# Destination blocks aligned to half groups in a four-layer graph network kernel

## The chip, the cores and the metric

The kernel runs on one core of a Trainium2 chip. The metric is the device time of one execution in microseconds (us). Three executions of the kernel before took 2282.65, 2286.11 and 2288.14 us; the median, 2286.11, is its time. A separate, profiled execution took 2289.18 us. The engines are PE (matrix products), DVE (vector), ACT (scalar functions), POOL (general, here also the issuer of indirect DMAs) and SP (issuer of plain DMAs). Each works through its own list of instructions, and semaphores order them among each other.

## The reference

A graph of 625 nodes with 512 features each and 20,000 edges goes through four layers. Each is `x = x + layer(relu(layernorm(x)))`. Cut to what each does with the edges:

```
# layer 0: mean over incoming edges, then one product
mean = segment_sum(x[src], dst) / max(count, 1)
out  = concat(x, mean) @ W.T + b
# layer 1, twice: relational convolution, 4 bases, 8 relations
m    = sum_b comp[etype, b] * (h @ basis[b])[src] * norm
out  = segment_sum(m, dst) + bias + h @ loop_w
# layer 2: tensor product messages, 1024 numbers for an edge
tpw  = silu-MLP(edge_attr_8) @ W4            # four weights of 128
m    = concat(w1*s0*y0, w4*<s1,y1>/sqrt3, w2*s0*y1, w3*s1*y0)
out  = lin(segment_sum(m, dst))
# layer 3: edge MLP, 512 numbers for an edge
h    = mish(concat(x[src], x[dst], edge_attr_64) @ W1 + b1)
agg  = segment_sum(mish(h @ W2 + b2), dst)
y    = layernorm(x + mish(concat(x, agg) @ W3 + b3) @ W4 + b4)
```

## The kernel before, in words

**Blocks, slots, tiles, groups.** The 625 nodes are 5 blocks (`NB`) of 125 (`BN`). The edges are sorted by the block of their destination; each edge gets a slot. A tile is 128 slots, a group (`TG` = 4 tiles, `SG` = 512 slots) is what layers 2 and 3 handle at a time. Each block's slots begin at a multiple of `SG`, so that all edges of a group end in one block, and there are `NG` = 44 groups, `NT` = 176 tiles. `block_of_group` says for each group which block it is; the pass reads it with a value load and adds to that block of `total`. An edge's record (80 floats: attributes, weight, source, destination) is written to its slot in `sorted_records` by an indirect DMA that POOL issues, one for each of 160 columns of 125 edges (`scatter_records`, L677 to L682). Only half of the records fit on chip at a time: columns 0 to 79 (`EARLY`) first, and the late ones come in by `late_records` on SP into the same room, after the early ones that stood there are scattered.

**Stages.** They follow each other, each in an `nc.Block()`; an engine's list in a stage is written out in the kernel, and the places below in that list are the order of the work.

- `place_edges` (to 65 us in the profiled execution): counts by bucket, slots, `block_of_group`.
- `order_pairs` (65 to 207): lists (source, destination) pairs for layers 0 and 1. Meanwhile POOL issues 64 of the scatters (`FIRST`, L482), then waits for `placed` and clears the tail of `pairs` (L484). DVE computes the layer norm's statistics of x (L656 to L663) in the middle of its last loop.
- `build_pairs` (207 to 403): the pair matrices. SP brings in late records of columns 0 to 63.
- `layer0` (403 to 467), `normalize` (to 480). POOL in layer 0: L1149, five scatters, five adds of a bias (L1154), eleven scatters.
- `relation_conv` twice (480 to 625.5, 625.5 to 792). In the first (c = 0) POOL issues the 80 late scatters, and SP loads the late records of columns 64 to 79 before its conv weights (L1281 to L1284). The second (c = 1) turns the sorted records into transposed attributes, in `UNITS` = 22 units of 8 tiles (L1450 to L1457 on DVE, L1394 on ACT, L1337 and L1384 on PE), beside its matrix products.
- `message_pass` (816 to 1321, layer 2), `edge_tables` (to 1387) and `edge_mlp_pass` (1387 to 2186, layer 3), `node_tail`.

**Message pass.** For each tile k of a group g, PE computes four path weights (`path_weights`, L1641 to L1643, bf16), one layer of the next group's MLP (`layer`, L1634, k < 3), and `scatter` (L1653, L1655): fp32 products of a one-hot matrix `hot` (slot to node of the block) with the message of 1024 columns, summed in PSUM over the group's four tiles in `sum_ps[g % 2]`. DVE makes the products for the messages from PSUM and the gathered rows (`paths`: L1745, L1750, L1756), the products with the record's vector and their sum over three components (`turn` L1721, `inner_first` L1729, `inner_second` L1734), `hot` (L1712), and adds the finished sum of group g-1 to `total` after tile 1 (`add`, L1769). ACT scales four pieces for each tile (L1689) and does the MLP's silu (L1682). POOL copies a group's source rows (L1601) and gathers them by four indirect DMAs (L1607), two groups ahead, in a ring of four.

**Edge pass.** A group has two units of two tiles. PE builds the first layer's input from `by_dst` rows of the group's block times the columns `hotT` (L1918), from the attributes (L1919, L1920) and the gathered source rows (L1923), multiplies by `w2` (L932), and scatters (L1946), summing over both units. DVE makes `hotT` by a comparison (`hot_columns`, L2022), `hot` (L2027), the mish pieces (L2035, L2040, L2046, L2058) and one add for each group (`add`, L2067). ACT does the exponentials and logarithms; POOL the low parts (L1873, L1878) and gathers.

Of the kernel before, what the change touches and what calls it, by code (L numbers as in the profile page):

```python
# [12 lines left out]
FP32 = mybir.dt.float32  # L13
# [14 lines left out]
SG = TG * P  # L28
RING = 4
NG = (EDGES + NB * (SG - 1)) // SG  # L30
NG += -NG % RING
# [14 lines left out]
FIRST = 64  # L46
# [23 lines left out]
def constants(pg):  # L70
# [19 lines left out]
    pg.block_of_group = pg.sb("block_of_group", [1, NG], I32)  # L90
# [37 lines left out]
    pg.scattered = pg.keep.enter_context(nc.semaphore("record_scattered"))  # L128
    pg.arrived = [pg.keep.enter_context(nc.semaphore(f"arrived{b}")) for b in range(RING * TG)]
# [31 lines left out]
def place_edges(pg):  # L161

    nc = pg.nc
    with ExitStack() as ctx:
# [18 lines left out]
        groups = pg.sb("groups", [P, NB], ctx=ctx)  # L183
        last_group = pg.sb("last_group", [P, NB], ctx=ctx)
# [4 lines left out]
        group_no = pg.sb("group_no", [P, NG], ctx=ctx)  # L189
        group_blk = pg.sb("group_blk", [P, NG], ctx=ctx)  # L190
        group_past = pg.sb("group_past", [P, NB - 1, NG], ctx=ctx)
# [11 lines left out]
                "rows_counted", "rows_summed", "ints_read", "weight_read", "weight_rounded", "weight_part", "weight_left", "tables_made", "tables_turned", "group_compared")}  # L203
# [25 lines left out]
        def _(pool):  # L229
# [6 lines left out]
            nc.gpsimd.iota(group_no[:, :], [[1, NG]], base=0, channel_multiplier=0,  # L236
                           allow_small_or_imprecise_dtypes=True).then_inc(sem["iota_done"], 1)
            pool.wait_ge(sem["group_compared"], 1)
            nc.gpsimd.tensor_tensor(group_past[:, 0:2, :], group_past[:, 0:2, :], group_past[:, 2:4, :],
                                    ALU.add).then_inc(sem["group_compared"], 1)  # L240
            pool.wait_ge(sem["group_compared"], 2)
            nc.gpsimd.tensor_tensor(group_blk[:, :], group_past[:, 0, :], group_past[:, 1, :],
                                    ALU.add).then_inc(sem["group_compared"], 1)
            pool.wait_ge(sem["group_compared"], 3)
            nc.gpsimd.tensor_copy(pg.block_of_group[:, :], group_blk[0:1, :])
            nc.gpsimd.tensor_copy(pg.block_of_tile[:, :].rearrange("p (g k) -> p g k", k=TG),
# [160 lines left out]
def order_pairs(pg):  # L407
# [8 lines left out]
    with ExitStack() as ctx:  # L416
# [2293 lines left out]
```

## Time and profile before

| stretch (us) | stage | length | PE busy | DVE busy | ACT busy | POOL busy |
|---|---|---|---|---|---|---|
| 0 to 65 | constants, place_edges | 65 | 1.7 | 52.8 | 12.9 | 8.3 |
| 65 to 207 | order_pairs | 142 | 106.6 | 115.5 | 78.5 | 115.1 |
| 207 to 403 | build_pairs | 196 | 158.5 | 171.8 | 151.1 | 146.5 |
| 403 to 480 | layer0, normalize | 77 | 60.2 | 55.1 | 14.0 | 45.5 |
| 480 to 625.5 | first convolution | 145.5 | 137.9 | 49.4 | 23.8 | 112.7 |
| 625.5 to 792 | second convolution | 166.5 | 147.8 | 59.9 | 42.8 | 0.0 |
| 816 to 1321 | message pass | 505 | 494.7 | 427.4 | 262.0 | 216.7 |
| 1387 to 2186 | edge pass | 799 | 769.4 | 709.4 | 550.6 | 679.1 |
| 2186 to 2287 | node tail | 101 | 66.2 | 27.7 | 22.2 | 12.5 |

The profiled execution took 2289.18 us; its span, from the first to the last instruction, is 2287.4 us, and the mean clock that PE was granted was 0.959 of full speed. A timeline row gives the start, the busy time, the engine, the line, the operation, what it writes and reads with shapes, the number of instructions taken together, and in brackets the idle time before it and what ended it. In the table of stretches a busy time is the engine's own within the stretch; time in which an indirect DMA is prepared by POOL counts as busy, the gap of about 0.3 us between two of them does not.

### The profile page before, as it was taken

To read this page: it belongs to the slowest core of one execution; us is meant where nothing else is said; L and a number is where in the kernel's file an instruction comes from. 1 tells how busy PE (TensorE), PEld (TensorE's weight loads), DVE (VectorE), ACT (ScalarE), POOL (GpSimd) and SP (SyncE) were. 2 spreads that over 40 slices of the span, in tenths; PEclk is the share of its full clock that TensorE was granted. 3 is DMA by queue.
4 is the path that set the end of the run, shared out by engine and by line. 5 is a ranking of instruction groups with operands and counts; after the bars stand their busy time and mean duration, and the time that the engine had idled before them with its cause. 6 is when DMAs were issued, how large, how long until landed. Compare 5 with 4: busy or idle time off the path is not lost. (4 is left out here: it accounts for less than half of the span.)

```text
span 2287.4 us, 35553 instructions
## 1 busy us (share of the span) xinstructions
PE 2009.2 (88%) x11336; PEld 1132.4 (50%) x11456; DVE 1708.3 (75%) x2399; ACT 1178.9 (52%) x1952; POOL 1349.6 (59%) x1068
## 2 busy tenths in 40 slices
PE   0894888879998779999999987999999999999875
PEld 0773777446565534444444453545555554555332
DVE  8995998743333558888888845999999999999623
ACT  1664777121122225555555524777677767777522
POOL 1787777747600054444444105898998989899530
PEclk9997999889999879999999999999999999999987
DMA  2411000222144245333333214322222222222000
GB/s 116 163 21 59 0 0 0 72 82 69 33 119 122 70 123 157 116 94 94 94 98 96 50 33 133 114 72 78 72 78 70 81 76 71 73 77 77 1 0 23
DMA packets 81683, 170.25 MB, mean 74 GB/s; under 512 B 17383, under 2 KB 43226, under 8 KB 80579
## 3 DMA queue, kind: packets, MB, share of 16 engines
q0 software_dynamic: 35840, 98.88, 16.0%
q1 hardware_dynamic: 45754, 70.25, 9.3%
q8 instruction: 48, 0.79, 0.1%
q14 instruction: 41, 0.34, 0.0%
HBM read 144.93 MB, written 23.98 MB: 74 GB/s over the span
## 5 line engine op out<-in xcount | busy, mean ns | idle before, releaser
L932 PE MATMUL e_two_ps<-w,e_first 128*128 128x512 bf16 x1342 | 405.4, 380 | 4.0 <-issue 0.2
L680 POOL DMA_INDIRECT sorted_records<-edge_record,slot_row x160 | 248.2, 1551 | 84.0 <-issue 55.2
L1689 ACT ACTIVATE u_msg<-u_t,slot_record 128x128 f32<-128x128 f32 x704 | 223.3, 390 | 93.2 <-DVE u_t L1745 93.1
L2349 POOL DMA_INDIRECT e_got<-src_table,e_idx x176 | 227.9, 1295 | 70.4 <-issue 34.8
L932 PE MATMUL e_two_ps<-w,e_first_low 128*128 128x512 bf16 x685 | 260.2, 380 | 0.6
L1873 POOL TENSOR_TENSOR e_first_low<-e_first 128x1024 bf16<-128x1024 f32 x88 | 248.4, 2823 | 12.6 <-DVE e_first L2046 12.6
L1607 POOL DMA_INDIRECT u_got<-up_table,u_idx x176 | 186.4, 1059 | 76.8 <-issue 42.9
L1878 POOL TENSOR_TENSOR e_msg_low<-e_act 128x1024 bf16<-128x1024 f32 x88 | 200.6, 2279 | 38.0 <-DVE e_act L2058 36.5
L932 PEld LDWEIGHTS e_two_ps<-w,e_first 128*128 128x128 bf16 x1408 | 134.4, 98 | 148.4 <-issue 2.2
L734 PE MATMUL pairs_ps<-cell_high,src_hot 128*128 128x144 bf16 x1180 | 153.6, 227 | 60.7 <-POOL cell_rest L758 38.6
L1653 PE MATMUL u_sum_ps<-u_msg,u_hot 128*125 128x512 f32 x352 | 185.2, 608 | 3.2 <-ACT u_msg L1689 3.1
L1655 PE MATMUL u_sum_ps<-u_msg,u_hot 128*125 128x512 f32 x352 | 180.6, 595 | 0.0
L2053 DVE TENSOR_TENSOR e_lin<-e_two_ps,bias 128x512 f32<-128x512 f32 x176 | 120.4, 684 | 63.6 <-PE e_two_ps L932 63.6
L2035 DVE SCALAR_TENSOR_TENSOR e_act<-e_act 128x1024 f32<-128x1024 f32 x88 | 160.9, 1828 | 5.9 <-ACT e_act L1971 5.9
L1976 ACT ACTIVATE e_act<-e_lin 128x1024 f32<-128x1024 f32 x88 | 93.0, 1057 | 125.0 <-DVE e_lin L2053 125.0
L1980 ACT ACTIVATE e_act<-e_act,log_bias 128x1024 f32<-128x1024 f32 x88 | 101.1, 1148 | 107.9 <-DVE e_act L2035 107.9
L734 PEld LDWEIGHTS pairs_ps<-cell_high,src_hot 128*128 128x128 bf16 x1180 | 115.8, 98 | 76.8 <-POOL cell_rest L758 74.5
L737 PE MATMUL pairs_ps<-cell_rest,src_hot 128*128 128x128 f16 x1180 | 153.1, 221 | 0.0
L1601 POOL COPY u_idx<-src_row 128x4 uint32<-128x4 uint32 x44 | 26.0, 592 | 194.4 <-DVEq L1760 171.1
L1436 DVE TENSOR_TENSOR pairs<-rc_mix,pairs 125x512 bf16<-125x512 f32 x40 | 27.7, 692 | 146.9 <-ACT pairs L1404 146.9
L1358 PE MATMUL rc_out<-pairs 125*125 125x512 bf16 x600 | 135.6, 379 | 1.2
L1682 ACT ACTIVATE u_hid<-u_mlp_ps 128x256 f32<-128x256 f32 x132 | 50.5, 383 | 146.4 <-PE u_mlp_ps L1634 146.4
(373 smaller groups left out, 4726.9 us busy)
## 6 DMA issues: line engine op xcount, KB each, us to landing
conv_w<-in_L_gnn_basis_dram SPq DMA_DIRECT2D x8, 1024.0 KB, 5.6
sorted_records<-pairs SPq DMA_DIRECT2D x5, 1408.0 KB, 10.9
later_w<-in_L_gnn_W_dram SPq DMA_DIRECT2D x6, 1024.0 KB
attr_parts<-h SPq DMA_DIRECT2D x22, 256.0 KB, 2.1
e_attrT<-attr_parts SPq DMA_DIRECT2D x44, 128.0 KB
e_dst_all<-dst_row SPq DMA_DIRECT2D x44, 125.0 KB
edge_record<-in_edge_floats_dram SPq DMA_DIRECT2D x1, 3125.0 KB
pairs<-in_edge_floats_dram SPq DMA_DIRECT2D x1, 3125.0 KB
```

The source lines that it names most:

```text
L680: pg.nc.gpsimd.indirect_dma_start(out=pg.sorted, out_offset=bass.IndirectOffsetOnAxis(ap=pg.slot_row[:, j:j + 1], axis=0), in_=pg.edge_rec ...
L734: nc.tensor.matmul(ps[h][:, sb, 0:(COEFS + 1) * CELL], hot, high[:, h, k, :, :].rearrange("p n d -> p (n d)"), start=(k == 0 and sb % 2 == ...
L737: last = nc.tensor.matmul(ps[h][:, sb, 0:COEFS * CELL], hot, rest[:, h, k, :, :].rearrange("p n d -> p (n d)"), start=False, stop=(k == 1 ...
L932: last = nc.tensor.matmul(out, lhsT, rhs, start=(n == 0), stop=(n == len(pairs) - 1))
L1607: nc.gpsimd.indirect_dma_start(out=got[:, b, :], out_offset=None, in_=tableU, in_offset=bass.IndirectOffsetOnAxis(ap=idx[:, r, k:k + 1], a ...
L1653: nc.tensor.matmul(sum_ps[h][0:BN, 0:D], hot[:, h * TG + k, :], msg[:, k, 0:D], start=(k == 0), stop=(k == TG - 1))
L1655: nc.tensor.matmul(sum_ps[h][0:BN, D:M], hot[:, h * TG + k, :], msg[:, k, D:M], start=(k == 0), stop=(k == TG - 1)).then_inc(scattered, 1)
L1689: last = nc.scalar.activation(msg[:, k, at * MUL:(at + 1) * MUL], t12[:, k % 2, of], ACT.Copy, scale=pg.record[:, bass.ds(t, 1), Y + m])
L1873: nc.gpsimd.tensor_tensor(first_low[:, r % 2, 2 * u:2 * u + 2, :], full, upper(full), ALU.subtract).then_inc(low1, 1)
L1878: nc.gpsimd.tensor_tensor(msg_low[:, u, :, :], act2[:, u, :, :], upper(act2[:, u, :, :]), ALU.subtract).then_inc(low2, 1)
L2035: nc.vector.scalar_tensor_tensor(out=act1[:, u, :, :], in0=act1[:, u, :, :], scalar=2.0, in1=act1[:, u, :, :], op0=ALU.add, op1=ALU.mult). ...
L2349: pg.nc.gpsimd.indirect_dma_start(out=self.got[:, r * TG + k, :], out_offset=None, in_=table, in_offset=bass.IndirectOffsetOnAxis(ap=self. ...
```

## The change

Blocks are aligned to a half group, 256 slots (`HG`), so a group's first and second half may belong to two blocks. The worst case needs fewer slots: `NG` = 42 groups (84 halves, `NH`), 168 tiles, 21 units in the second convolution. What depends on the block is now by half: `block_of_half`, the sums of the message pass (`sum_ps[k // 2]`, two tiles each), the sums of the edge pass (`sum_ps[u]`, one unit each), and the edge pass's rows by destination, which are taken in two products of 256 columns where one of 512 was.

In the message pass ACT copies each half group's sum from PSUM to `part` (`take_sum`), after tiles 0 and 2, and POOL adds `part` to `total` (`add`), after its gathers 0 and 2; DVE's add is gone. In the edge pass DVE adds for each unit, and ACT makes `hotT` by an absolute value and a relu (`hot_columns`), where DVE compared. The loop by four groups becomes `group_by_group`, which the message pass used already.

In the ordering stage POOL issues 52 scatters (`FIRST`) and its clear of the tail goes to ACT; DVE's statistics of x move ahead of its wait for `placed`. Layer 0 then has the bias adds first and 12 scatters (to `BESIDE` = 64), and the first convolution 16 + 52 + 28 = 96. SP there loads the weights 1 and 2 before the late records. Late scatters count on a semaphore of their own.

```diff
+TH = TG // 2
+HG = TH * P
-NG = (EDGES + NB * (SG - 1)) // SG
-NG += -NG % RING
+NH = (EDGES + NB * (HG - 1)) // HG
+NG = -(-NH // 2)
+NH = 2 * NG
-FIRST = 64
+FIRST = 52
+BESIDE = 64
...
 # order_pairs, POOL
             scatter_records(pg, range(0, FIRST))
-            pool.wait_ge(placed, 1)
-            nc.gpsimd.memset(pairs[:, HOTS:], 0.0)
 # order_pairs, ACT
+            act.wait_ge(placed, 1)
+            clear(pairs[:, HOTS:])
...
 # layer0, POOL
-            scatter_records(pg, range(FIRST, FIRST + 5))
             pool.wait_ge(bias_in, 16)
             for b in range(NB):
                 nc.gpsimd.tensor_tensor(pg.x[:, b, :], pg.x[:, b, :], bias[:, :], ALU.add).then_inc(biased, 1)
-            scatter_records(pg, range(FIRST + 5, EARLY))
+            scatter_records(pg, range(FIRST, BESIDE))
...
 # relation_conv, c == 0, SP
-                sp.wait_ge(pg.scattered, 16 * EARLY)
-                late_records(pg, sp, FIRST, EARLY)
                 for m in range(1, BASES + 2):
                     load_conv_weight(pg, room, sp, m)
+                    if m == 2:
+                        sp.wait_ge(pg.scattered, 16 * EARLY)
+                        late_records(pg, sp, FIRST, EARLY)
...
 # relation_conv, c == 0, POOL
+                scatter_records(pg, range(BESIDE, EARLY))
                 pool.wait_ge(pg.record_in, 16)
                 scatter_records(pg, range(EARLY, EARLY + FIRST))
...
 # message_pass, POOL
+            def add(n):
+                at = nc.gpsimd.value_load(pg.block_of_half[0:1, bass.ds(n, 1)], min_val=0, max_val=NB - 1)
+                pool.wait_ge(summed, n + 1)
+                if n >= 1:
+                    pool.wait_ge(added, n)
+                into = total[:, bass.ds(at, 1), :].rearrange("p a d -> p (a d)")
+                nc.gpsimd.tensor_tensor(into, into, part[:, n % 2, :], ALU.add).then_inc(added, 1)
...
                 for k in range(TG):
                     if more:
                         gather((r + 2) % RING, k)
+                    if k == 0 and at > 0:
+                        add(2 * g - 1)
+                    if k == 2:
+                        add(2 * g)
...
 # message_pass, PE
+                if k % TH == 0 and g >= 1:
+                    pe.wait_ge(summed, 2 * (g - 1) + k // TH + 1)
                 if k == 0:
-                    pe.wait_ge(added, g + 1)
                     pe.wait_ge(hot_ready, g + 1)
...
 # message_pass, ACT
+            def take_sum(n):
+                act.wait_ge(scattered, TH * (n + 1) + 2 * TG)
+                if n >= 2:
+                    act.wait_ge(added, n - 1)
+                nc.scalar.copy(part[:, n % 2, :], sum_ps[n % 2][0:BN, :]).then_inc(summed, 1)
...
                 for k in range(TG):
                     vector_paths(g, r % 2, k)
                     if k < 3 and at < LAST:
                         layer(g + 1, 1 - r % 2, k)
+                    if k == 0 and at > 0:
+                        take_sum(2 * g - 1)
+                    if k == 2:
+                        take_sum(2 * g)
...
 # message_pass, DVE
-                    if k == 1 and at > 0:
-                        add(g - 1, 1 - r % 2)
...
 # edge_mlp_pass, PE
                     for part in range(2):
-                        rows = by_dst[:, bass.ds(at, 1), part, cols].rearrange("p b d -> p (b d)")
-                        nc.tensor.matmul(ps, rows, hotT[:, h, :], start=(part == 0), stop=False)
+                        for half, at in enumerate(blocks):
+                            rows = by_dst[:, bass.ds(at, 1), part, cols].rearrange("p b d -> p (b d)")
+                            slots = slice(half * HG, (half + 1) * HG)
+                            nc.tensor.matmul(pre_ps[u][:, i, slots], rows, hotT[:, h, slots],
+                                             start=(part == 0 and half == 0), stop=False)
...
 # edge_mlp_pass, ACT
+                if u == 0 and at + 3 < NG:
+                    hot_columns(g + 3, (r + 3) % 2)
+
+            def hot_columns(g, h):
+                act.wait_ge(attr_in[h], (g - h) * 16 + 32)
+                act.wait_ge(pre_ready, 2 * g - 2 + 2 * RING)
+                nc.scalar.activation(off_lane[:, h, :], dst_all[:, h, :], ACT.Abs,
+                                     bias=gathers.minus_lane[:, 0:1]).then_inc(offs_made, 1)
+                act.wait_ge(offs_made, g + 1)
+                nc.scalar.activation(hotT[:, h, :], off_lane[:, h, :], ACT.Relu, bias=pg.ones[0:BN, 0:1],
+                                     scale=-1.0).then_inc(hotT_ready, 1)
```

## Rows read from the trace of the kernel before

**Rows 1.** The profile page's first line.
```profile
span 2287.4 us, 35553 instructions
```

**Rows 2.** Busy us (instructions): PE, PEld, DVE, ACT, POOL; granted clock, DMA share, GB/s.
```profile
480.00:625.50 145.50, 137.85 (x620) 86.11 (x620) 49.41 (x44) 23.82 (x32) 112.74 (x80) 0.96 0.24 64
...
816.00:1321.00 505.00, 494.69 (x1466) 227.85 (x1496) 427.37 (x838) 261.97 (x837) 216.72 (x221) 0.98 0.36 102
...
1387.00:2186.00 799.00, 769.44 (x4487) 388.57 (x4576) 709.43 (x660) 550.61 (x529) 679.11 (x385) 0.99 0.26 74
```

**Rows 3.** Timeline of the ordering stage: start, us, instruction [idle before <- releaser].
```profile
155.69 0.40 DVE L605 COPY h<-pair_slots_ps 128x236 f32<-128x236 f32 x1 [3.30 <-PE pair_slots_ps L514]
175.18 3.06 DVE L656 BATCH_NORM_STATS2 x_stats<-x 125x6 f32<-125x512 f32 x5
186.91 0.64 DVE L673 TENSOR_TENSOR pair_rest<-hT,pair_high 128x472 f16<-128x472 f32 x1
199.19 4.25 POOL L484 MEMSET pairs<- 128x4960 f32 x1
207.31 0.83 ACT L769 ACTIVATE src_off<-iota_src,hT 128x640 f16<-128x640 f16 x1 [21.19 <-ACTq L765]
```

**Rows 4.** Layer 0: the queries of line L1169, and POOL's timeline.
```profile
L1169 DVE TENSOR_TENSOR w<-w x2: 2598/4989/7380, 411.3 to 419.3; 128x2048 bf16<-128x2048 f32 x2
  PEld first_out L1106: 2.4, 1
...
417.97 6.24 POOL L1154 TENSOR_TENSOR x<-x,bias 125x512 f32<-125x512 f32 x5
```

**Rows 5.** Timeline of POOL and DVE at both ends of the first convolution.
```profile
480.62 1.19 POOL L680 DMA_INDIRECT sorted_records<-edge_record,slot_row  x1 [27.41 <-DMA edge_record<-in_edge_floats_dram]
...
621.03 1.19 POOL L680 DMA_INDIRECT sorted_records<-edge_record,slot_row  x1 [0.30 <-issue]
624.55 0.68 DVE L1493 TENSOR_TENSOR hT<-rc_mix,hT 128x500 bf16<-128x500 f32 x1 [1.00 <-ACT hT L1413]
```

**Rows 6.** Timeline of DVE at the last unit of the second convolution.
```profile
777.41 0.43 DVE L1450 CAST h<-edge_record 128x512 bf16<-128x512 f32 x1 [2.46 <-PE attr_ps L1337]
```

**Rows 7.** Timeline of the message pass, one group; then the add of two groups.
```profile
1010.87 1.12 PE L1653 MATMUL u_sum_ps<-u_msg,u_hot 128*125 128x512 f32 x2
1016.13 0.59 PE L1634 MATMUL u_mlp_ps<-u_hid,u_w 128*128 128x256 f32 x2
1018.93 1.02 PE L1653 MATMUL u_sum_ps<-u_msg,u_hot 128*125 128x512 f32 x2
1016.76 0.38 ACT L1682 ACTIVATE u_hid<-u_mlp_ps 128x256 f32<-128x256 f32 x1 [1.25 <-PE u_mlp_ps L1634]
1017.04 1.26 ACT L1689 ACTIVATE u_msg<-u_t,slot_record 128x128 f32<-128x128 f32 x4
1018.48 0.69 DVE L1729 TENSOR_TENSOR u_q<-u_turned 128x512 f32<-128x512 f32 x1
1019.81 0.42 DVE L1745 TENSOR_TENSOR u_t<-u_tp_ps,u_got 128x256 f32<-128x256 f32 x1
1018.56 0.66 POOL L1601 COPY u_idx<-src_row 128x4 uint32<-128x4 uint32 x1 [4.56 <-DVEq L1760]
...
1100.76 1.21 DVE L1769 TENSOR_TENSOR total<-total,u_sum_ps 125x1024 f32 x1
1111.90 1.21 DVE L1769 TENSOR_TENSOR total<-total,u_sum_ps 125x1024 f32 x1
```

**Rows 8.** Line queries of L1971 and L2035: least, median and greatest ns.
```profile
L1971 ACT ACTIVATE e_act<-e_pre_ps x88: 999/1001/1023, 1392.4 to 2140.0; 128x1024 f32<-128x1024 f32 x88
...
L2035 DVE SCALAR_TENSOR_TENSOR e_act<-e_act x88: 1217/1781/4704, 1393.5 to 2141.3; 128x1024 f32<-128x1024 f32 x88
```

**Rows 9.** Timeline of PE: the first scatter of two units of the edge pass.
```profile
1601.67 0.39 PE L1946 MATMUL e_sum_ps<-e_act,e_hot 128*128 128x512 bf16 x1
...
1610.36 0.39 PE L1946 MATMUL e_sum_ps<-e_act,e_hot 128*128 128x512 bf16 x1
```

More of the change, by code:

```diff
@@ L527, in _, with clear @@
         def _(act):
+            def clear(to):
+                nc.scalar.activation(to, pg.ones[:, 0:1].broadcast_to(list(to.shape)), ACT.Copy, scale=0.0)
             size = (HOTS - CLEARED) // (BATCHES - WAITED)
@@ L603, in _ @@
                                   .broadcast_to([P, NB, P])).then_inc(names_made, 1)
+            dve.wait_ge(pg.x_in, 16)
+            for b in range(NB):
+                last = nc.vector.bn_stats(out=pg.x_stats[:, b, :], in_=pg.x[:, b, :])
+            last.then_inc(x_chain, 1)
+            dve.wait_ge(x_chain, 1)
+            for b in range(NB):
+                last = nc.vector.bn_aggr(out=x_mv[:, b, :], in_=pg.x_stats[:, b, :])
+            last.then_inc(x_chain, 1)
+            dve.wait_ge(x_chain, 2)
+            nc.vector.tensor_scalar(x_sd[:, :], x_mv[:, :, 1], EPS, None, ALU.add).then_inc(x_var, 1)
             dve.wait_ge(placed, 1)
@@ L824, in gather_sems @@
     for b in range(ring * TG):
-        pg.landed[b] += 16 * (NG // ring)
+        pg.landed[b] += 16 * len(range(b // TG, NG, ring))
     return sems
@@ L1267, in units_of @@
             after = lambda i: i + (i > NB) + (i > 2 * NB)
-            return range(after(n), after(n + 1))
+            return range(min(after(n), UNITS), min(after(n + 1), UNITS))
         @block.sync
@@ L1903, in first_layer @@
                 h = r % 2
-                at = nc.tensor.value_load(pg.block_of_group[0:1, bass.ds(g, 1)], min_val=0, max_val=NB - 1)
+                blocks = [nc.tensor.value_load(pg.block_of_half[0:1, bass.ds(2 * g + half, 1)], min_val=0,
+                                               max_val=NB - 1) for half in range(2)]
                 pe.wait_ge(mish1_ready, n + 1)
@@ L1941, in scatter @@
                 pe.wait_ge(hot_ready, g + 1)
-                if u == 0:
-                    pe.wait_ge(added, g + 1)
+                pe.wait_ge(added, n + 1)
                 for i in range(2):
                     for part, half in enumerate((upper(act2[:, u, i, :]), msg_low[:, u, i, :])):
-                        last = nc.tensor.matmul(sum_ps[r % 2][:, :], hot[:, (r % 2) * TG + 2 * u + i, :],
-                                                half, start=(u == 0 and i == 0 and part == 0),
-                                                stop=(u == 1 and i == 1 and part == 1))
+                        last = nc.tensor.matmul(sum_ps[u][:, :], hot[:, (r % 2) * TG + 2 * u + i, :],
+                                                half, start=(i == 0 and part == 0), stop=(i == 1 and part == 1))
                 last.then_inc(scattered, 1)
@@ L2098, in _ @@
             dve.sem_inc(two_ready, 4 * 2)
-            for g in range(2):
-                hot_columns(g, g)
             for n in range(AHEAD):
@@ L2109, in _ @@
             steps(dve, body)
-            add(NG - 1, (NG - 1) % 2)
+            for n in range(UNITS - 3, UNITS):
+                add(n, n % 2)
 class MessageWeights:
```

154 lines of the change are left out of this document (64 added, 90 removed).

## The prediction, made before the changed kernel was run

> **What bounds the kernel now.** I read the page's head first: 2287.4 us of span inside a profiled execution of 2289.18, so 1.8 us lie around the span [rows 1]. This execution stands 3.1 us above the median of 2286.11; I add my sum to the median. Then busy time by stage [rows 2]. The message pass (816 to 1321) and the edge pass (1387 to 2186) keep PE busy for 495 of 505 us and 769 of 799 us: PE bounds both, a group costs PE's sum, and a group less saves it. DVE is busy for 427 of 505 us in the message pass, so a second copy of its 1.21 us add per group [rows 7] would leave almost nothing free there. The first convolution (480 to 625.5) is different: PE is busy for 138 of 145.5 us, yet POOL runs scatters from its first microsecond to 622.2, and all other work ends only at 625.2 [rows 5]. The ordering stage ends on POOL alone: DVE's last instruction there ends at 187.55, POOL clears a buffer until 203.44, and ACT, idle for 21.19 us, begins the next stage only at 207.31 [rows 3]. So a stage's end holds back every engine, and I take it as a barrier in each stage.
>
> **Ordering.** 12 scatters leave POOL. One is 1.19 us and a gap of 0.30 [rows 5], so POOL's last ends at 199.19 - 12 x 1.49 = 181.3. The clear (4.25 us on POOL) goes to ACT, which is idle when its condition comes and delays nothing later than DVE's chain. DVE's layer norm statistics (3.06 for the five L656 and about 0.6 for the short steps after them) move ahead of a wait on which DVE stood idle for 3.30 us [rows 3]. The end goes from 203.44 to between 187.5 (no gain from the move) and 183.9 (all of it); I take 185.4: -18 (-16 to -19.5).
>
> **Placement and layer 0.** Five vectors in the placement stage are 84 wide instead of 44: +0.2. In layer 0, POOL's five bias adds ended at 424.2, and DVE's second weight split, which began at 419.31, took 7.38 us where the first took 2.60 [rows 4]; PE waited 2.4 us for it [rows 4]. The adds now come before the scatters and end some 7 us earlier. If the wait goes, 2.4; if what is next (PE's own work) takes over, 0: I take -1.5.
>
> **First convolution.** The 12 scatters, and 4 that layer 0 did before, come back here: 96 for 80. POOL's 80 took 622.22 - 480.62 = 141.6, of which 80 x 1.49 = 119.2 are their own and 22.4 are stretches in which they stood behind DVE's weight splits. 96 x 1.49 + 22.4 = 165.4, so POOL ends near 646. DVE's end, 625.2, is 3 us behind POOL's today and 21 ahead of it then. The cover for these scatters is used up: 16 x 1.49 = 23.8 minus the 3.0 that was left is +21 (17, if some of the splits no longer meet a scatter, to 25). SP loads the second weight before the late records, which can shorten a wait of the weight chain: worth nothing while POOL ends 21 us after everybody else. Within SP's queue the late records now stand behind two weight loads; POOL needs them only after 68 more scatters, 100 us in. **Second convolution.** One of 22 conversion units goes. Before the last one DVE stood idle for 2.46 us for PE [rows 6]; with its share of the instructions I take -2.5 (0 to -3.7).
>
> **Message pass.** Today's group is 1111.90 - 1100.76 = 11.14 us [rows 7]; 44 of them are 490.2. DVE's add goes, but PE and not DVE was the bound, so this saves nothing by itself. Added: ACT copies a half group's sum (125x1024) from PSUM twice per group, and POOL adds it to the total twice. A 1024 wide ACT read from PSUM is 1.00 us, about 0.90 before the next can start [rows 8]. POOL's add of 512 elements is 6.24/5 = 1.25 us [rows 4]; scaled it is 2.36 for 1024 after taking off a fixed 0.2 (bounds: 1.9 to 2.9, what POOL's 1024 wide instructions of the edge pass take). The Trainium skill, page "GPSIMD Engine Reference", section "Performance versus the Vector engine", gives 4497 ns for 2048 elements of such an add; an estimate from it is 2.25 us, and the sum below would be about 5 us less by it.
>
> Where does it land? Let M be the start of the third MLP matmul, 1016.13. ACT's silu starts at M+0.63, its next instruction at M+0.91 and lasts four scalings, 1.26 us; PE starts the last scatter at M+2.80 [rows 7]. In the new order the copy takes the slot at M+0.91, the scalings run from M+1.81 to M+3.08, and with 0.15 for the signal PE starts at M+3.23: 0.43 late, every group. That alone makes a group 11.57.
>
> The copy ends near M+1.91, so POOL's add starts at about 1018.10, 0.38 us before DVE's L1729 (1018.48), which reads two operands from SBUF. Two places of this trace show what then happens. DVE's L1169 took 7.38 for 2.60 while POOL's adds ran [rows 4], and L2035 of the edge pass has a median of 1.78 against a least of 1.22 and up to 4.70 [rows 8]. And in this very group POOL's tiny index copy (4 elements) starts at 1018.56 and ends at 1019.22, with L1729's end [rows 7]. The two engines exclude each other for a whole instruction. The Trainium skill says the same, page "SBUF — State Buffer", section "Who interferes with whom": a DVE instruction with two SBUF inputs and a GpSimd instruction that reads SBUF lock each other out, and the one issued first holds the pair; by that rule, the trace agrees.
>
> So L1729 waits for POOL until 1018.10 + 2.36 = 1020.46. It and L1734 take 0.72 and 0.61 to their successors, and L1745 of the next group starts at 1021.79 instead of 1019.81. From there ACT's scalings (0.45 to start, 1.28) and the signal (0.15) put the next first scatter at M+7.53. PE's own work from that scatter to the next M is two scatters of 1.72, two path products of 0.65 and a layer of 0.43: 5.17 (today the whole way is 5.26, 1010.87 to 1016.13). The period is 12.70. 42 x 12.70 = 533.4, plus 2.2 for a last copy and add with nothing beside them, minus 490.2: +45.4. Lower bound of the group 11.0 (PE's sum, all hidden); upper 13.6.
>
> POOL itself: 216.72/44 = 4.9 busy [rows 2] and 1.7 of gaps, plus 2 x 2.36 = 11.3 us: over today's period, under 12.70. Its gathers are two groups ahead, and stay ahead.
>
> **Edge pass.** A unit is 1610.36 - 1601.67 = 8.69 [rows 9], two per group; two groups less are -34.8. The half group matmuls have the same number of columns in total. The hot columns move from DVE to ACT, as two instructions of about 0.7 (from 0.83 at 640 wide [rows 3]) per group, against (799 - 551)/42 = 5.9 us of ACT's idle time per group [rows 2]. DVE loses one instruction and gains another 0.67 add. The first columns now wait for ACT's table load, +1.2. I take -33.5 (-35 to -28).
>
> **Sum.** -18 + 0.2 - 1.5 + 21 - 2.5 + 45.4 - 33.5 = +11.1, so 2297. The alignment saves about 36 us in three stages, the moved scatters are about even, and the message pass gives more than all of it back.
>
> **Rivals.** (a) The engines don't get in each other's way where it matters, and only ACT's 0.43 stays: 42 x 11.57 + 2.2 - 490.2 = -2.1, in all -36: 2250. For it: the margin at 1018.1 is only 0.4 us, and DVE without its add has 1.2 us more slack earlier in the group; if the adds fell between 1012 and 1014.6, or on DVE's PSUM-reading instructions, which show no stretch, all would be hidden. Against it: DVE's q steps stand right where the copy ends, and nothing moves them earlier, since L1707 waits for the same silu. (b) L1729 gets in first: POOL's add then starts at its end, and L1734 waits for all 2.36 us. Period about 13.4: 42 x 13.4 + 2.2 - 490.2 = +75, in all +41: 2327. It decides from the point at which the copy ends 0.4 us later than I have it, as it would with a copy of 1.3 us. This is the case that is clearly slower. (c) The message pass is as I say, but the scatters hide: if the first convolution's splits absorb them or the barrier does not bind, 21 less: 2276. Against it is ACT's restart after POOL's clear [rows 3]. (d) Others: POOL saturates on its gathers too, or ACT's new functions in the edge pass reload tables: 2340 and more.
>
> **Chances.** Forecast 0.40 (its own range 2283 to 2308), (a) 0.22, (b) 0.20, (c) 0.11, (d) 0.07. No change means within 0.2%, 4.6 us, which is what this measurement can tell. Faster: all but a little of (a) and (c), and a few hundredths of the forecast's low end: 0.36. Same: mostly the forecast with its sum 7 us too high: 0.13. Slower: the rest, 0.51. The range 2245 to 2332 takes in (a), (b) and (c).
>
> **What would show it.** In the new trace: the next stage after ordering starts near 189; POOL's last scatter of the first convolution ends near 646 and PE starts the next one just behind; the third MLP matmul recurs every 12.7 us in the message pass; L1729 has a median near 3 us or starts 2 us late, and the ACT copy sits between silu and the scalings; edge units stay at 8.69. A message group at 11.6 or less, or L1729 at 0.69 beside POOL's add, would prove me wrong, and so would a PE that goes on at 625 with scatters still running.

## The result: 10.8% slower, and where the time is in the new profile

The changed kernel takes 2531.48 us (median of 4 runs, 2530.88 to 2535.19) against 2286.78 for the kernel before beside it: a ratio of 1.1076, 95% interval 1.1057 to 1.1095. The profiled execution has a span of 2530.2 us, 242.8 more than before [rows 1].

The profile's first line, then stretches of the changed kernel (busy us of PE, PEld, DVE, ACT, POOL, then granted clock, DMA share, GB/s): first convolution, message pass, edge pass, to be held against [rows 2].

```profile
span 2530.2 us, 35530 instructions
...
454.50:623.40 168.90, 135.98 (x621) 85.53 (x622) 50.20 (x44) 23.92 (x32) 132.11 (x96) 0.89 0.24 62
824.90:1363.80 538.90, 476.11 (x1387) 211.39 (x1414) 435.62 (x751) 319.35 (x879) 410.67 (x287) 0.99 0.31 89
1438.30:2433.70 995.40, 805.41 (x4619) 414.43 (x4704) 641.58 (x630) 579.12 (x586) 645.39 (x366) 0.93 0.20 57
```

The edge pass kept PE busy for 769 of 799 us before; now it is 805 of 995. It has two groups less to do there; its busy time is longer by 36 us all the same, at a granted clock of 0.93 for 0.99, and it is idle for 190 us where it was for 30. The message pass had 495 of 505 and has 476 of 539. By the events that begin and end each stage in both traces:

| stage | before | after | difference | forecast |
|---|---|---|---|---|
| to the start of build_pairs | 207.3 | 186.7 | -20.6 | -17.8 |
| build_pairs, layer 0, normalize | 272.6 | 267.9 | -4.7 | -1.5 |
| first convolution | 145.6 | 168.8 | +23.2 | +21 |
| second convolution | 166.7 | 163.1 | -3.6 | -2.5 |
| to the message pass | 36.5 | 38.5 | +2.0 | 0 |
| message pass | 492.9 | 538.8 | +45.9 | +45.4 |
| to the edge pass | 66.6 | 74.6 | +8.0 | +1.2 |
| edge pass | 797.4 | 994.7 | +197.3 | -34.7 |
| tail | 101.8 | 97.2 | -4.6 | 0 |

The forecast is the prediction's sum laid out by these stages. Six of the nine terms are within about 3 us, two are off by 7 and 5. One, the edge pass, is off by 232 us and has the wrong sign.

Timeline of the changed kernel at the end of the ordering stage, and at the end of the first convolution.

```profile
155.19 4.33 ACT L532 ACTIVATE pairs<-ones 128x4960 f32<-128x4960 f32 x1 [5.16 <-issue]
184.30 0.66 DVE L679 TENSOR_TENSOR pair_rest<-hT,pair_high 128x472 f16<-128x472 f32 x1 [0.22 <-ACT pair_high L567]
186.72 0.83 ACT L776 ACTIVATE src_off<-iota_src,hT 128x640 f16<-128x640 f16 x1 [2.45 <-ACTq L772]
...
619.99 1.18 POOL L686 DMA_INDIRECT sorted_records<-edge_record,slot_row  x1 [0.30 <-issue]
623.37 3.22 PE L1352 MATMUL rc_out<-conv_w_parts,hT 128*125 128x512 bf16 x7 [28.49 <-PEq L1232]
```

The clear is on ACT at 155.19. DVE is now last, ending at 184.96, and ACT restarts at 186.72 after 2.45 us of idle time where it had 21.19 [rows 3]. The first convolution ends with POOL: its last scatter ends at 621.17, and PE, idle for 28.49 us, begins the next stage at 623.37. Before, POOL and DVE ended there within 3 us of each other [rows 5].

One group of the message pass in the changed kernel: ACT's copy, POOL's add, DVE's first q step and the next product, and PE's scatter with what it waited for (idle before, releaser).

```profile
1000.37 1.01 ACT L1710 COPY u_part<-u_sum_ps 125x1024 f32<-125x1024 f32 x1
1001.56 2.34 POOL L1615 TENSOR_TENSOR total<-total,u_part 125x1024 f32 x1 [1.22 <-ACT u_part L1710]
1001.80 2.65 DVE L1753 TENSOR_TENSOR u_q<-u_turned 128x512 f32<-128x512 f32 x1
1005.09 0.42 DVE L1769 TENSOR_TENSOR u_t<-u_tp_ps,u_got 128x256 f32<-128x256 f32 x1
1002.69 1.09 PE L1666 MATMUL u_sum_ps<-u_msg,u_hot 128*125 128x512 f32 x2 [0.27 <-ACT u_msg L1702]
1006.97 1.09 PE L1666 MATMUL u_sum_ps<-u_msg,u_hot 128*125 128x512 f32 x2 [1.06 <-ACT u_msg L1702]
```

This is the order worked out beforehand: copy, POOL's add at 1001.56, then the q step (`inner_first`, the first addition of the sum over three components), issued 0.24 us later. It lasts 2.65 us for 0.69 and ends 0.55 us after POOL's add. L1769, which was L1745 in [rows 7], comes 2 us late, and PE stands for 1.06 us before the next group's first scatter and 0.27 before the last one of this group.

The query of the edge pass's scatter line in the changed kernel: what its engine waited for (us, times); then a unit of the edge pass on DVE and PE. L2059 is DVE's widening, one of the mish pieces: `x (x + 2)` on 1024 columns, with both inputs in SBUF.

```profile
its engine sat idle before it (us, times) until:
  DVE total L2091: 164.8, 78
```

```profile
1801.68 0.39 PE L1962 MATMUL e_sum_ps<-e_act,e_hot 128*128 128x512 bf16 x1 [2.09 <-DVE total L2091]
1811.55 1.78 DVE L2059 SCALAR_TENSOR_TENSOR e_act<-e_act 128x1024 f32<-128x1024 f32 x1
1811.84 0.38 PE L939 MATMUL e_two_ps<-w,e_first_low 128*128 128x512 bf16 x1
1813.25 0.68 DVE L2077 TENSOR_TENSOR e_lin<-e_two_ps,bias 128x512 f32<-128x512 f32 x1
1813.85 0.67 DVE L2091 TENSOR_TENSOR total<-total,e_sum_ps 125x512 f32 x1
1814.67 0.39 PE L1962 MATMUL e_sum_ps<-e_act,e_hot 128*128 128x512 bf16 x1 [2.45 <-DVE total L2091]
...
1825.63 0.39 PE L1962 MATMUL e_sum_ps<-e_act,e_hot 128*128 128x512 bf16 x1 [2.10 <-DVE total L2091]
```

PE's last product of the second layer's first half starts at 1811.84. DVE's bias for it (L2077) starts at 1813.25, held back by the widening before it, and only then comes the add, which ends near 1814.5; PE's scatter starts at 1814.67 after 2.45 us of idle time. The next unit has the same again, and the query counts it 78 times for 84 units, 2.1 us each. The period of two units is 1825.63 - 1801.68 = 23.95 us, where it was 17.38. PE's busy time, granted clock, DMA share and GB/s in one such stall and in two stretches behind it:

```profile
1799.50:1801.60 2.10, 0.09 (x1) 1.00 0.08 29
1801.70:1806.20 4.50, 4.50 (x14) 0.62 0.34 87
1806.20:1812.00 5.80, 5.75 (x43) 1.00 0.06 24
```

The stall at full clock is followed by 4.5 us in which the clock is 0.62 of full, the lower level (1.2 GHz) for most of it, and PE's products start 0.41 to 0.43 us apart instead of 0.22. Not every such stall has this behind it. Over the whole pass 47 of the 78 units with the wait took 10.94 to 11.01 us and 30 took 12.63 to 12.67; the unit shown, 12.99 with a wait of 2.45, is the longest, the other waits are 2.09 to 2.14 (one 3.03). So the wait costs about 2.3 us in each unit, 10.95 for 8.69, and the lower clock another 1.7 in 31 of them.

### The profile page after: what moved, and what is told of

It is laid out like the page before. It is cut to its first block and busy times, and to the rows that moved or that the text cites. A ratio compares the mean times of both kernels' runs of the same rounds, so it can differ in the third digit from the quotient of the medians.

```text
span 2530.2 us, 35530 instructions
## 1 busy us (share of the span) xinstructions
PE 2025.4 (80%) x11394; PEld 1142.8 (45%) x11507; DVE 1648.9 (65%) x2287; ACT 1272.3 (50%) x2058; POOL 1511.6 (60%) x1123
## 5 line engine op out<-in xcount | busy, mean ns | idle before, releaser
L939 PE MATMUL e_two_ps<-w,e_first 128*128 128x512 bf16 x1261 | 423.6, 415 | 4.7 <-issue 0.5
L1891 POOL TENSOR_TENSOR e_msg_low<-e_act 128x1024 bf16<-128x1024 f32 x84 | 239.9, 2855 | 269.6 <-DVE e_act L2082 269.5
L2077 DVE TENSOR_TENSOR e_lin<-e_two_ps,bias 128x512 f32<-128x512 f32 x168 | 114.9, 685 | 329.3 <-PE e_two_ps L939 329.3
L939 PE MATMUL e_two_ps<-w,e_first_low 128*128 128x512 bf16 x672 | 275.7, 410 | 0.0
L1886 POOL TENSOR_TENSOR e_first_low<-e_first 128x1024 bf16<-128x1024 f32 x84 | 237.9, 2832 | 15.0 <-DVE e_first L2070 15.0
L1605 POOL DMA_INDIRECT u_got<-up_table,u_idx x168 | 209.0, 1244 | 60.2 <-POOL u_idx L1599 32.5
L1615 POOL TENSOR_TENSOR total<-total,u_part 125x1024 f32 x84 | 197.8, 2354 | 70.8 <-ACT u_part L1710 70.7
L1666 PE MATMUL u_sum_ps<-u_msg,u_hot 128*125 128x512 f32 x336 | 178.6, 613 | 58.2 <-ACT u_msg L1702 58.2
L2369 POOL DMA_INDIRECT e_got<-src_table,e_idx x168 | 175.0, 1042 | 67.2 <-issue 33.7
L1962 PE MATMUL e_sum_ps<-e_act,e_hot 128*128 128x512 bf16 x168 | 67.1, 399 | 180.0 <-DVE total L2091 164.8
L1668 PE MATMUL u_sum_ps<-u_msg,u_hot 128*125 128x512 f32 x336 | 172.2, 594 | 0.0
L2059 DVE SCALAR_TENSOR_TENSOR e_act<-e_act 128x1024 f32<-128x1024 f32 x84 | 150.0, 1785 | 13.1 <-issue 11.2
```

The source lines that it names most:

```text
L939: last = nc.tensor.matmul(out, lhsT, rhs, start=(n == 0), stop=(n == len(pairs) - 1))
L1605: nc.gpsimd.indirect_dma_start(out=got[:, b, :], out_offset=None, in_=tableU, in_offset=bass.IndirectOffsetOnAxis(ap=idx[:, r, k:k + 1], a ...
L1615: nc.gpsimd.tensor_tensor(into, into, part[:, n % 2, :], ALU.add).then_inc(added, 1)
L1666: nc.tensor.matmul(sum_ps[k // TH][0:BN, 0:D], hot[:, h * TG + k, :], msg[:, k, 0:D], start=(k % TH == 0), stop=(k % TH == TH - 1))
L1668: nc.tensor.matmul(sum_ps[k // TH][0:BN, D:M], hot[:, h * TG + k, :], msg[:, k, D:M], start=(k % TH == 0), stop=(k % TH == TH - 1)).then_i ...
L1886: nc.gpsimd.tensor_tensor(first_low[:, r % 2, 2 * u:2 * u + 2, :], full, upper(full), ALU.subtract).then_inc(low1, 1)
```

## Experiments

All are timed beside the kernel before, whose median was 2286.8 to 2288.9 us; the changed kernel took 2531.5.

**1. The add one statement earlier (e1_add_first).** In DVE's `body` of the edge pass:

```diff
+                if at >= 2 or (at == 1 and u == 1):
+                    add(n - 3, 1 - u)
                 if not last:
                     bias(n + 1, 1 - u, 0)
-                if at >= 2 or (at == 1 and u == 1):
-                    add(n - 3, 1 - u)
```

> Changed kernel, one statement moved: in the edge pass DVE makes the add of unit n-3 before it waits for PE's first half of unit n+1's second layer (bias(n+1, 0)), not after. Theory A (the new wait is a loop: PE's scatter waits for an add that stands on DVE behind a product which PE makes just before that scatter): the 2.1 to 2.5 us stall of PE per unit goes, and with it PE's drop to the lower clock after it; a unit goes from 11.98 to 8.69 us, 84 x 3.3 = 276 less: 2255 us. Rival B (the 256 column products, the hot columns on ACT or the unrolled loop are what costs): the same 2531 within 5 us.

Measured: 2427.43 us, 104 less than the changed kernel. The place of the add matters, but 276 was expected. DVE and PE in this run:

```profile
1805.17 1.78 DVE L2059 SCALAR_TENSOR_TENSOR e_act<-e_act 128x1024 f32<-128x1024 f32 x1
1806.88 0.68 DVE L2091 TENSOR_TENSOR total<-total,e_sum_ps 125x512 f32 x1
1807.70 0.39 PE L1962 MATMUL e_sum_ps<-e_act,e_hot 128*128 128x512 bf16 x1 [1.50 <-DVE total L2091]
...
1818.06 0.39 PE L1962 MATMUL e_sum_ps<-e_act,e_hot 128*128 128x512 bf16 x1 [1.49 <-DVE total L2091]
```

The add no longer stands behind the bias, but the widening, 1.78 us, is ahead of it, and PE waits 1.50 us in each unit; a unit takes 10.36, all at full clock (1.00 from 1600 to 2000). Rival B falls (it gave 2531), and theory A was too narrow about what stands ahead of the add. Experiments 3 and 4 have expected totals worked out from the 2255 us that theory A gave here, and experiment 6 from the 2286 us of theory A in experiment 5; what can be compared there are the gains, not the totals.

**2. Unit sums alone in the kernel before (e2_before_unit_sums).**

```diff
-                if u == 0:
-                    pe.wait_ge(added, g + 1)
+                pe.wait_ge(added, n + 1)
...
-                        last = nc.tensor.matmul(sum_ps[r % 2][:, :], hot[:, (r % 2) * TG + 2 * u + i, :],
+                        last = nc.tensor.matmul(sum_ps[u][:, :], hot[:, (r % 2) * TG + 2 * u + i, :],
...
-                if u == 1:
-                    if at >= 1:
-                        add(g - 1, (r - 1) % 2)
+                if at >= 2 or (at == 1 and u == 1):
+                    add(n - 3, g - 2 + u, 1 - u)
```

> Kernel before, with one part of the change alone: the edge pass sums and adds per unit, with the add at the place where the change has it. No half blocks, no hot columns on ACT, no unrolled loop. Theory A: every unit gets the same stall, 88 x 3.3 = 290 more than before: 2575 us. Rival B: only one more 0.67 us add per group on DVE, which has 0.6 us free per unit: 2286 to 2292.

Measured: 2622.12 us, ratio 1.1453 (1.1429 to 1.1476): 334 more than before. With no half blocks, no shorter slots and no work on ACT, this one part brings the whole loss and more. The query of its scatter line says what it waits for. PE and its weight loads are counted together here; PE's own waits are 226.8 us in 82. In the trace of before, POOL was the only releaser of any size at this line.

```profile
its engine sat idle before it (us, times) until:
  DVE total L2065: 317.4, 118
```

**3. The q steps out of POOL's way (e3_q_early).** On top of experiment 1, in the message pass:

```diff
                     if k == 2 and more:
+                        inner_first(g + 1, 1 - r % 2)
+                        inner_second(g + 1, 1 - r % 2)
                         hot_group(g + 1, 1 - r % 2)
-                if more:
-                    inner_first(g + 1, 1 - r % 2)
-                    inner_second(g + 1, 1 - r % 2)
```

> As e1_add_first, and in the message pass DVE makes the two q steps right after the third tile's turn, before hot, and not at the end of the group. Theory C (the q steps stand behind POOL's add for its whole 2.35 us, and that delays the next first scatter): the q steps take 0.69 again, the group goes from 12.53 to about 11.57 (only ACT's copy is left in PE's way), 42 x 0.96 = 40 less than e1: 2215. Rival D (PE's waits in this pass come from the ACT copy ahead of the scalings alone): no difference to e1 within 5 us, or slower by the 1.3 us that the fourth tile's product now waits for DVE: up to +40.

Measured: 2394.41 us, 33.0 less than experiment 1. The line of the first q step, least, median and greatest ns, in the changed kernel and in this one:

```profile
L1753 DVE TENSOR_TENSOR u_q<-u_turned x42: 692/2652/2887, 823.6 to 1346.1; 128x512 f32<-128x512 f32 x42
```

```profile
L1753 DVE TENSOR_TENSOR u_q<-u_turned x42: 691/692/693, 820.2 to 1306.8; 128x512 f32<-128x512 f32 x42
```

Nothing was taken away: the copies and POOL's adds are as they were, the q step only runs at another time, and it takes 0.69 again for 2.65. The group goes from 12.75 to 11.83 us. 42 x 0.92 = 39 was to be had, and 33 came. Of the 0.7 that is left over 11.14, DVE's list has a part: from 900 to 1250, PE's weight loads wait 27.4 us, in 29 waits, for DVE's `u_hid_low` of the fourth tile, which now stands behind the q steps. What ACT's copy has in it was not taken apart.

**4. DVE adds both halves (e4_dve_adds).** On top of experiment 1; ACT's copies and POOL's adds are gone, and DVE has

```diff
+                    if k == 1 and at > 0:
+                        add(2 * g - 1)
+                    if k == 2:
+                        add(2 * g)
```

> As e1_add_first, and in the message pass neither ACT's copies nor POOL's adds: DVE adds each half group's sum from PSUM itself, after tiles 1 and 2. Theory C: with no POOL add there is nothing to lock out; DVE carries 1.2 us more per group than before the change and 10.9 of 11.1 us in all, so the fourth tile comes late by about a microsecond or less: 11.5 to 12.0 per group, 20 to 43 less than e1: 2212 to 2235. Rival E (DVE is full, so the second add costs its whole 1.21 us on top of PE's 11.0 to 11.1 and more for its place): 12.4 or more per group, no gain over e1 (2255).

Measured: 2378.05 us, 49.4 less than experiment 1 where 20 to 43 was expected, a group of 11.68. Better than expected, since the stage also ends faster: the pass itself is 44 us shorter, and the way behind it 5. With POOL last, PE restarts 6.1 us after POOL's add (1363.71 to 1369.79 in the changed kernel), here 0.3 us after DVE's. From the start of the message pass's last scatter to the edge pass's first product it is 69.8 us, where it is 77.0 in experiment 1, 78.8 in the changed kernel and 68.6 before.

**5. The add at the start of the unit (e5_add_start).** Changed kernel, with

```diff
+                if at >= 1:
+                    add(n - 2, u)
                 widen2(n, u)
...
-                if at >= 2 or (at == 1 and u == 1):
-                    add(n - 3, 1 - u)
```

> Changed kernel; in the edge pass DVE adds unit n-2 at the very start of its unit n, ahead of all its waits for ACT and PE (in e1_add_first it still stood behind the final, widen and final steps of the same unit, and PE waited 1.5 us per unit for it). Theory A (only the add's place in DVE's list makes PE wait): PE's wait for the total goes to 0, a unit takes 8.69 us as before the change, 84 x 1.68 = 141 less than e1's 2427: 2286 us, or 2299 by the stage's lengths. Rival F (with a sum of its own per unit the scatter, the add and the one-hot rows cost more than DVE has free, at any place): unit at 9.3 or more, 2340 or more.

Measured: 2411.78 us, 16 less than experiment 1. A miss: 141 less was expected. PE's wait for the total is gone altogether, and 44 waits for POOL's `e_msg_low` (L1891), 106.0 us, stand in its place (234.5 in 89 with those of its weight loads). DVE, POOL and PE in this run:

```profile
1805.44 4.64 DVE L2059 SCALAR_TENSOR_TENSOR e_act<-e_act 128x1024 f32<-128x1024 f32 x1
1805.24 1.90 POOL L1891 TENSOR_TENSOR e_msg_low<-e_act 128x1024 bf16<-128x1024 f32 x1
1807.09 1.90 POOL L1886 TENSOR_TENSOR e_first_low<-e_first 128x1024 bf16<-128x1024 f32 x1
1807.19 0.40 PE L1962 MATMUL e_sum_ps<-e_act,e_hot 128*128 128x512 bf16 x1 [2.72 <-POOL e_msg_low L1891]
```

DVE issues its widening 0.2 us after POOL's subtraction began. POOL's next subtraction follows at once, and DVE gets its turn only behind both: 4.64 us for 1.22. Of the 84 widenings 38 are like this one and 46 take 1.21 to 1.33; in 44 units another DVE step, L2064, takes 2.50 to 2.54 for 1.23. In the kernel before, the widening had a median of 1.78 [rows 8]:

```profile
1608.02 2.20 POOL L1878 TENSOR_TENSOR e_msg_low<-e_act 128x1024 bf16<-128x1024 f32 x1
1609.51 1.78 DVE L2035 SCALAR_TENSOR_TENSOR e_act<-e_act 128x1024 f32<-128x1024 f32 x1
1610.18 2.87 POOL L1873 TENSOR_TENSOR e_first_low<-e_first 128x1024 bf16<-128x1024 f32 x1
```

It got in between POOL's two, and POOL's second took 2.87 for 1.90. This edit changes two things, the add's place and the unit it adds (n-2 for n-3). The times at which the two engines meet shifted with it, and the two held back steps took most of what the removed wait had given. That the shift came from the add's place is argued here; experiment 9 keeps the place and changes the unit alone.

**6. Adds on DVE, the one-hot matrix where DVE is idle (e6_dve_adds_hot_mid).** Experiments 4 and 5 together, and `hot_group(g + 1, 1 - r % 2)` at k == 1 for k == 2.

> As e5_add_start, with the message pass of e4_dve_adds (DVE adds both half sums from PSUM, no copy on ACT, no add on POOL), and the one-hot matrix made after tile 1, where DVE stood idle for 0.46 us, and not between the second add and the fourth tile. The adds alone gave 49 less than e1. If what is left of e4's 11.68 us per group is the fourth tile waiting for DVE, the move takes another 0.2 to 0.5 us per group: 8 to 21 less. In all 2215 to 2232. If DVE's sum per group (10.9 us) is the bound and not the order, no more than e4's gain: 2237 or more.

Measured: 2337.90 us, 74 less than experiment 5; with 49 from the adds, the move gave 25, a little more than the 8 to 21 expected. The profiles agree: the message pass is 24.1 us shorter than in experiment 4. A stretch of its message pass:

```profile
900.00:1250.00 350.00, 348.89 (x1048) 160.61 (x1068) 336.57 (x630) 189.23 (x596) 160.87 (x157) 1.00 0.35 100
```

PE is busy for 348.89 of 350 us. A group takes 11.14 us from one `hot` to the next, as in the kernel before (the 11.07 of experiment 11's expectation is 465 us over 42, but from the first tile's product to the last's it is 41.75 groups). DVE carries 336.57 of 350, where it had 427 of 505 [rows 2], so it was the order and not the amount.

**7 and 8. Where the scatters stand (e7_beside_72, e8_first_64).** Experiment 6 with `BESIDE = 72`, and with `FIRST = 64`, `BESIDE = 80`.

> As e6, but 20 scatters in layer 0 and 88 in the first convolution, for 12 and 96. Theory G (the first convolution ends with POOL's last scatter, and layer 0 has 12 us at its end in which POOL does nothing): 8 x 1.49 = 12 less than e6. Rival H (a scatter costs the same where DVE is busy in layer 0, or the stage's end is not POOL's): within 4 us of e6.

> As e6, with the scatters as they were before the change: 64 in the ordering stage, 16 in layer 0, 80 in the first convolution; the clear on ACT and the early statistics stay. The forecast had the moved scatters about even: the ordering stage 18 longer less the clear's 4.25 (14), layer 0 up to 4 longer, the first convolution 21 shorter. So 3 less than e6, between -8 and +4. If ordering's gain were independent of POOL's scatters, 20 less.

Measured: 2329.70 and 2327.74 us, 8 and 10 less than experiment 6. The first lies between theory G (12) and rival H (4 at most), the second gained 2 us more than its expectation allowed. With 72, the first convolution got 10.5 us shorter (168.7 to 158.2), but the way from layer 0 to it 4.7 longer: of the 8 scatters more, 11.9 us, about 5 were hidden there. With 64 and 80, the ordering stage is 16.7 longer and the first convolution 23.8 shorter. So POOL's scatters set the end of both stages, and by the stages' lengths the scatters as they were before the change are about 7 us better; another 3.5 us of the 10 lie before the message pass, where runs whose code is the same up to there differ by as much (34.9 to 38.6 us). The difference between 7 and 8 is inside the spread of their runs.

**9. One number in the changed kernel (e9_lag_2).** The add stands where the change has it, but handles the unit before:

```diff
-                if at >= 2 or (at == 1 and u == 1):
-                    add(n - 3, 1 - u)
+                if at >= 1:
+                    add(n - 2, u)
```

> Changed kernel, with one number changed: DVE's add in the edge pass stands where the change has it, after the first bias of unit n+1, but adds unit n-2 and not n-3. PE scatters unit n-2 in its unit n before the second half of the second layer, so its sum is done by then, and the add that the scatter of unit n-2 waits for (unit n-4) now stands one whole DVE unit earlier. Theory A2 (the loop is one of distance: an add one unit too late; and e5_add_start left it but lost its gain since the add ahead of DVE's first widening shifted POOL's two subtractions against DVE's widenings): PE's wait for the total is 0, DVE's widening stays at 1.78, a unit is 8.7 us, 111 less than e5: 2300. Rival I (with sums per unit DVE and POOL fall out of step at any distance): a unit of 9.9 or more, 2400 or more.

Measured: 2303.40 us, ratio 1.0074 (1.0053 to 1.0095): 228 less than the changed kernel. The scatter line's releasers (PE and its weight loads; before, POOL's `e_msg_low` had 57.1 us in 97 waits at this line), and PE's scatters of two units:

```profile
its engine sat idle before it (us, times) until:
  POOL e_msg_low L1891: 58.1, 92
...
1702.75 0.39 PE L1962 MATMUL e_sum_ps<-e_act,e_hot 128*128 128x512 bf16 x1
1711.45 0.39 PE L1962 MATMUL e_sum_ps<-e_act,e_hot 128*128 128x512 bf16 x1
```

No wait for the total is listed; 1711.45 - 1702.75 = 8.70 us. DVE's widening has its median of 1.78 again. Theory A2 holds: 2300 was expected, and the forecast for the whole change, which knew no such loop, was 2297.

**10. The same in the kernel before (e10_before_lag_2).** Experiment 2 with `add(n - 2, g - 1, u)`.

> As e2_before_unit_sums (kernel before with sums and adds per unit in the edge pass), but adding unit n-2 in the same place. Theory A2: 0.3 us of DVE's time per unit, which is hidden: the 334 us go, 2286 to 2295. Rival I: 2350 or more.

Measured: 2286.00 us (10 runs), ratio 0.9995 (0.9981 to 1.0009). Sums and adds per unit cost nothing at this distance; at the other one they cost 334 us. Rival I falls here and in experiment 9.

**11. What works, together (e11_all).** Experiment 9, the message pass of experiment 6, `FIRST = 56`, `BESIDE = 72`.

> As e9_lag_2, with the message pass of e6_dve_adds_hot_mid (465 us for 42 groups, 11.07 each, against 490 before the change), and 56 scatters in the ordering stage, 16 in layer 0, 88 in the first convolution. Theory: e8's 2327.7 less the edge pass's 111, less 3 or 4 for the scatters: 2213. If the edge pass does not mend, 2324.

Measured: 2219.17 us, ratio 0.9707 (0.9685 to 0.9728), 67.6 less than the kernel before. Stretches of its message and edge passes, PE's busy time first:

```profile
900.00:1250.00 350.00, 350.00 (x1070) 160.70 (x1069) 336.23 (x629) 190.21 (x599) 159.62 (x156) 1.00 0.35 99
1500.00:2000.00 500.00, 498.65 (x3205) 273.95 (x3204) 439.74 (x431) 392.71 (x400) 441.86 (x258) 1.00 0.27 76
```

## Why the prediction was wrong

**What bounds the kernel, ordering, second convolution:** right, each within about 3 us; more was saved than forecast. DVE's end in the ordering stage was put at 185.4 and came at 184.96; the other 2 us are the restart, 1.8 us after DVE's end where it was 3.9 after POOL's clear. The first convolution's barrier was right: +21 forecast, +23.2 measured, and experiments 7 and 8 move its end with the number of scatters. Rival (c), that they hide, falls.

**Layer 0: the size was near, the way there was not.** The bias adds were to end some 7 us earlier. They began late, after 7.58 us of waiting for their DMA, and ended 19.5 us into the stage where it was 21.1. The weight split took its short time all the same, because now it was DVE that came first. POOL's five adds and DVE's two splits, in the changed kernel:

```profile
L1160 POOL TENSOR_TENSOR x<-x,bias x5: 1267/1282/3632, 392.9 to 397.8; 125x512 f32<-125x512 f32 x5
L1175 DVE TENSOR_TENSOR w<-w x2: 2607/2626/2646, 390.1 to 397.7; 128x2048 bf16<-128x2048 f32 x2
```

POOL's last add, at 397.8, is the one of 3.63 us: it stood behind the split that DVE had issued at 397.69.

**Message pass: right in size and mechanism.** The period was to be 12.70 and is 12.75; the stage +45.4 and is +45.9. That the q step stands behind POOL's add is shown by experiment 3 (moved away, 33 us come back with POOL's work unchanged) and by experiment 4 (taken away, 49). Rivals (a) and (b) fall: POOL's add was first, by 0.24 us where 0.38 was worked out, and DVE's step waited for its end (2.34 - 0.24 = 2.10 us, then 0.55 more, 2.65 in all). By the rule of the Trainium skill ("SBUF — State Buffer", "Who interferes with whom") the one issued first keeps the SBUF ports that the two engines share for its whole instruction, and the other is blocked; the trace agrees. The wait can last longer than one instruction. In experiment 5 DVE, waiting since 1805.44, did not get in when POOL's first ended at 1807.14, but after the second. The prediction's own [rows 4] have it too: DVE's split of 7.38 us, issued at 419.31, began its 2.60 us of work only when POOL's bias adds, four of which were still to end, had finished at 424.2. The prediction read these rows as "a whole instruction".

**Edge pass: the failed step.** The prediction said: "DVE loses one instruction and gains another 0.67 add", and took -33.5. It costed the sums per unit as work and never followed the wait that comes with them. PE's scatter of unit n-2 waits for the add of unit n-4, because each sum buffer is now used in every second unit and not every fourth. DVE had that add one place behind the bias for unit n, and the bias waits for the product that PE makes directly before the scatter. So PE, DVE and PE again stood in one line within each unit: 2.1 to 2.5 us, then the clock. In the kernel before, the add at this place was wanted only two units later, since the scatter of a group waits for the add of the group before the last. Experiments 2 and 10 differ only in whether unit n-3 or n-2 is added, and by 336 us; 9 gives back 228 of the changed kernel's 245. What is left, +16.6, is 5.5 more than the forecast's +11.1, and this nearness is in part luck: in experiment 9's profile, whose span is 13.4 us above the profile before, the edge pass with the loop gone saves 29.0 us for 34.7, and the way between the passes costs 6.2 for 1.2, while the ordering stage, layer 0, the second convolution, the way to the message pass and the tail are 11.5 us better than forecast in all. Where the edge pass's 5.7 us are was not looked into; its unit in the middle is 8.70.

None of the rivals was this one. The case "(d) Others" had 0.07 and named POOL's gathers, and table loads in the edge pass; a wait of PE for DVE was not among them, although what it takes to see it (the order of `body` on DVE and on PE) is in the code beside the line that was changed. The range's upper end, 2332, was missed by 199 us.

**Left open.** Why PE restarts 6.1 us after POOL's last add where it is 0.3 after DVE's: the ordering stage before also restarted 3.9 us after POOL's clear, but the convolution only 2.2 after POOL's scatter. Experiment 9 has the 6.1 us again. No run takes it apart. What decides in experiment 5 that POOL's second subtraction goes ahead of DVE's waiting one, where in the kernel before DVE got in between, is not settled either. Nor is why the same stall is followed by the lower clock in some units and not in others. The 5 us of the tail weren't looked into.

## What to carry to other kernels

When a change has a buffer used again after fewer steps than before, take the new wait on it, find the instruction that ends it in its own engine's list, and ask what each instruction ahead of that one waits for: if one of them waits for what the waiting engine did last, the two run one after the other, whatever the busy shares say. Count the distance in iterations, before and after. And where two engines exclude each other, it is the order of issue within tenths of a microsecond that has a price, so a long instruction is best placed where the other has nothing of that kind to run.

## What the runs showed of the hardware

- POOL's tensor add of 125x1024 floats from SBUF had a median of 2.35 us (2.36 was estimated from 512 elements) and held back a DVE add with two SBUF inputs by 1.96 us (median 2.65 for 0.69 in experiment 3). ACT's copy of the same size from PSUM took 0.99 to 1.01 in all 84 cases.
- Where POOL instructions followed each other without a gap, a waiting DVE instruction stood behind two of them in 38 of 84 units of experiment 5 (4.64 us for 1.22), and behind the bias adds of layer 0 until the last had ended (7.38 for 2.60). In the kernel before it mostly got in between two (1.78).
- DVE products with an input in PSUM (L1769, L1774, L1780) kept their times, 0.42, 0.61 and 0.28, in a pass with 84 of POOL's adds.
- A stall of 2.1 us of PE was followed by 4.5 us at a granted clock of 0.62, one of 2.45 us by none. In the changed kernel's edge pass 31 of 78 such units were longer by the lower clock, 12.65 us for 10.95; with 1.50 us of stall in each unit (experiment 1) the clock stayed at 1.00 from 1600 to 2000, and the whole kernel's mean was 0.963, for 0.940 in the changed one.
- PE restarted 6.1 us after POOL's last tensor add of a stage (changed kernel and experiment 9), 3.9 after POOL's clear, 2.2 after its last indirect DMA and 0.3 after DVE's last add.
- ACT's clear of 4960 columns took 4.33 us, POOL's memset of them 4.25 [rows 3].
